# Adding gathered rows inside the gather's own transfer, in the second layer of a graph network

## The reference, cut to what matters

```python
h = max(layernorm(x), 0)
x = x + L0(h, edges)          # attention over edges; L0 itself returns h + agg @ Wo.T + bo
h = max(layernorm(x), 0)
x = x + L1(h, edges)          # weighted graph convolution, then two dense layers
# in L1: msgs = (h @ W)[dst] * norm, summed over the edges of each src
```

## Time and profile before

| | |
|---|---|
| median of 3 runs | 1908.72 us (1906.43 to 1911.76) |
| the profiled execution | 1886.7 us, of which the span from first to last instruction is 1885.1 us |
| stage 1 (about 183 to 710 us of the span) | PE nearly always busy |
| stage 2 (about 712 to 1066 us) | 25 quads |
| stage 3 (about 1066 to 1885 us) | PE nearly always busy |
| granted TensorE clock, mean | 0.931 of full speed |

### The profile page before, as it was taken

One profiled execution on the slowest core, in us unless ns is written; L12 is line 12 of the kernel. 1 busy time (PEld: TensorE's weight loads), 2 busy tenths in 40 slices (PEclk: granted clock), 3 DMA queues, 4 the chain that ended last, 5 costly groups with the idle time before them and its releaser, 6 DMA issues.

```text
span 1885.1 us, 30557 instructions
## 1 busy us (share of the span) xinstructions
PE 1625.4 (86%) x6531; PEld 1087.2 (58%) x6531; DVE 1430.1 (76%) x5731; ACT 1185.6 (63%) x2297; POOL 1216.8 (65%) x849
## 2 busy tenths in 40 slices
PE   4927999999999985676675349999999999999999
PEld 2314666666666653454454126666666666666666
DVE  7955777777777747877776487888888888888873
ACT  4924666666666631222222268899998989899984
POOL 2032888878788736888887765666666666666660
PEclk9967999999999997878878669999999999999999
DMA  6996666666666664655556589999999999999981
GB/s 231 418 404 235 182 179 183 194 181 177 193 188 178 176 189 101 123 109 108 119 107 136 96 199 263 249 268 264 271 270 270 269 267 271 268 270 271 270 234 75
DMA packets 150749, 398.56 MB, mean 211 GB/s; under 512 B 21586, under 2 KB 60060, under 8 KB 150700
## 3 DMA queue, kind: packets, MB, share of 16 engines
q1 hardware_dynamic: 89388, 264.75, 41.7%
q0 software_dynamic: 56416, 115.46, 32.5%
q10 hardware_dynamic: 4896, 17.83, 2.4%
HBM read 217.73 MB, written 180.23 MB: 211 GB/s over the span
## 4 chain that ended last, share of the span: by engine, by line
PE 51%; POOL 23%; DMA 8%; DVE 7%; issue 6%; SPq 1%; ACTq 1%; ACT 1%; POOLq 0%; DVEq 0%
PE bank L1314 9%; POOL sums_dram L514 9%; PE bank L1427 8%; PE bank L1416 8%; POOL kept L588 5%; PE bank L1321 5%; DMA out_dram<-cg 4%; PE bank L1351 4%; PE bank L1307 4%; POOL b_rs L510 4%; POOL cg L518 4%; PE bank L1255 4%; DVE cg L984 3%; DMA sums_dram<-ub,sidx 2%; PE bank L1295 2%
## 5 line engine op out<-in xcount | busy, mean ns | idle before, releaser
L1416 PE MATMUL bank<-kept,w 128*128 128x512 f32 x784 | 356.4, 598 | 0.0
L1427 PE MATMUL bank<-w_sb,kept 128*128 128x256 f32 x1568 | 354.3, 379 | 0.0
L588 POOL TENSOR_TENSOR kept<-kept 128x1024 f32<-128x1024 f32 x98 | 232.2, 2370 | 180.5 <-DVE cg L984 180.5
L1427 PEld LDWEIGHTS bank<-w_sb,kept 128*128 128x128 f32 x1568 | 297.9, 190 | 81.9 <-issue 46.4
L514 POOL DMA_INDIRECT sums_dram<-ub,sidx x148 | 243.1, 1643 | 76.8 <-issue 43.0
L1380 PE MATMUL bank<-cg,en 128*128 128x256 f32 x386 | 131.7, 485 | 124.1 <-ACT cg L1153 62.2
L510 POOL TENSOR_TENSOR b_rs<-b_ve,minus_half 128x8 f32<-128x8 f32 x102 | 208.7, 2047 | 28.7 <-DVE b_ve L1001 28.7
L1416 PEld LDWEIGHTS bank<-kept,w 128*128 128x128 f32 x784 | 142.8, 192 | 143.1 <-issue 143.0
L1191 ACT ACTIVATE kept<-kept,b_nb,b_rs 128x256 f32<-128x256 f32 x392 | 202.3, 589 | 21.5 <-DVE b_nb L974 21.5
L1181 ACT ACTIVATE kept<-kept,b_nb,b_rs 128x256 f32<-128x256 f32 x392 | 202.3, 589 | 11.0 <-DVE b_nb L974 11.0
L1314 PE MATMUL bank<-qkv_w,zT 128*128 128x512 f32 x392 | 192.7, 614 | 19.0 <-ACT zT L1070 19.0
(11 more groups left out here) (200 smaller groups left out, 3362.2 us busy)
## 6 DMA issues: line engine op xcount, KB each, us to landing
sums_dram<-cg SPq DMA_DIRECT2D x162, 512.0 KB, 5.4
kept<-in_x_dram SPq DMA_DIRECT2D x97, 512.0 KB, 5.7
kept<-sums_dram POOLq DMA_DIRECT2D x97, 512.0 KB, 10.0
cg<-sums_dram SPq DMA_DIRECT2D x97, 512.0 KB, 8.6
out_dram<-cg SPq DMA_DIRECT2D x97, 512.0 KB, 9.8
sums_dram<-cg ACTq DMA_DIRECT2D x34, 512.0 KB, 8.5
row_d<-in_dst_dram SPq DMA_DIRECT2D x48, 128.0 KB, 3.6
row_k<-keys_dram SPq DMA_DIRECT2D x24, 256.0 KB, 4.6
```

The costliest lines, as they stand in the source:

```text
L588: pool.tensor_tensor(X1[k.slot(8)], X[k.slot(4)], H[k.slot(2)], ALU.add).then_inc(g_xh, 1)
L1416: ins = pe.matmul(bank[:, 2 + m, :], w01[:, c, m * P:(m + 1) * P], hT[k.slot(2)][:, c * GN:(c + 1) * GN], start=(c == 0), stop=(c == KC - 1))
L1427: ins = pe.matmul(to, rT[k.slot(2)][:, c * GN + j * P:c * GN + (j + 1) * P], w2_sb[:, c, :], start=False, stop=(c == KC - 1), skip_group_c ...
```

## The change

The four gathers of a quad write straight onto `kept[:, Q*p + i, :]` as accumulating indirect DMAs. `C0` is no longer written or read. DVE still waits for the gathers' semaphore at the same place, then raises `n_x1` by itself instead of through the addition.

```diff
@@ -514,6 +514,10 @@
                 pool.indirect_dma_start(sums, bass.IndirectOffsetOnAxis(idx, 0), rows, None,
                                         bounds_check=bound, compute_op=ALU.add).then_inc(done, 16)
 
+            def gather_add(to, table, idx, bound, done):
+                pool.indirect_dma_start(to, None, table, bass.IndirectOffsetOnAxis(idx, 0), bounds_check=bound,
+                                        compute_op=ALU.add).then_inc(done, 16)
+
             def gather(to, table, idx, bound, done):
                 pool.indirect_dma_start(to, None, table, bass.IndirectOffsetOnAxis(idx, 0), bounds_check=bound,
                                         oob_is_err=True).then_inc(done, 16)
@@ -562,7 +566,7 @@
                     if p >= 2:
                         pool.wait_ge(n_x1, p - 1)
                     for i in range(chunks(Step(p))):
-                        gather(C0[p % 2][:, i, :], sums0, node_i[:, Q * p + i, 0:1], last_row, n_c0[p % 2])
+                        gather_add(kept[:, Q * p + i, :], sums0, node_i[:, Q * p + i, 0:1], last_row, n_c0[p % 2])
                 k = p - 2
                 if 0 <= k < NQ:
                     pool.wait_ge(n_UB, k + 1)
@@ -908,8 +912,7 @@
                         dve.wait_ge(n_c0[q], 16 * Q * (a.off // 2) + 16 * n)
                     else:
                         dve.wait_ge(n_c0[q], a.turns(2, 16 * Q))
-                    dve.tensor_tensor(quad(kept, a, slice(None)), quad(kept, a, slice(None)), C0[q][:, 0:n, :],
-                                      ALU.add).then_inc(n_x1, 1)
+                    dve.sem_inc(n_x1)
                     dve.wait_ge(n_sel, a.value(1))
                     dve.tensor_tensor(quad(norm, a), quad(found, a), quad(ew_f, a), ALU.mult).then_inc(n_norm, 1)
                     pass_on(dve, (n_x1, a.value(1)))
```

## The result

The changed kernel takes 1931.0 us (median of 4 runs, 1927.3 to 1935.7) against 1907.9 for the kernel before on the same chip: a ratio of 1.0132, 95% interval 1.0113 to 1.0150. That is some 25 us slower; the two medians alone are 23 us apart. The forecast was slower, +33 us and 1942 us, with a range of 1893 to 1958.

A forecast was written before the change was run, and what follows sets the result against it. POOL's issuing of indirect DMAs was taken to bound stage 2. Dearer gathers (+44.4 us) less cheaper scatters (12.9), plus 1.3 at the start and 0.4 at the end, gave +33.2 us: 1942 us, range 1893 to 1958.

The forecast's parts named there:

- What bounds the stage: Stage 2 is bound by how fast POOL issues indirect DMAs: 8 a quad, 13.93 us a quad.
- The gather's price: Stage 2, POOL: each accumulating gather takes 1.64 us, 0.555 us more for each of 80 gathers, 44.4 us.
- Rival 3: The accumulation costs part of it, the new gather taking 1.2 to 1.45 us: 1904 to 1927 us; chance 0.09.
- rival 1: The accumulating gather costs POOL no more than the plain one, so only savings are left: -14.5 us, 1894 us; chance 0.17.
- The scatters' saving: Stage 2, POOL: without the DVE addition the scatters' mean falls from 1.781 to about 1.62 us, 12.9 us saved.
- The start and the end: Stage 2's first quad costs +1.3 us; its last quad, after the steady stretch, +0.4 us.
- Sum: 31.5 us in the stretch, 1.3 at the start and 0.4 at the end: +33.2 us, 1942 us.
- Rival 2: Another DVE instruction, the counting L902, takes the addition's place in holding POOL: +46 us, 1955 us; chance 0.13.
- Rival 4: The landings of gathers or scatters become the bound, a few us a quad: +60 us, 1969 us; chance 0.03.

The follow-up runs named there:

- plain scatter: Kernel before, with the scatters of stage 2 into `sums1` writing their rows instead of accumulating them: 1876.3 us, ratio 0.9833.
- run with both: Changed kernel, with DVE still doing an addition of the same shape (`kept + kept` into the unused `C0`): 1932.6 us, ratio 1.0139.
- one input: Kernel before, its DVE addition L911 replaced by three statistics instructions of one SBUF input each, results unused: 1885.4 us, ratio 0.9887.
- split addition: Kernel before, its DVE addition L911 cut into four instructions of 256 elements, same result: 1881.5 us, ratio 0.9876.
- longer code: Kernel before, with 30 tiny DVE memsets put in front of stage 2 that compute nothing: 1875.7 us, ratio 0.9925.
- phase: Changed kernel plus an unused DVE addition placed some 1.2 us later, behind two unused statistics instructions: 1923.9 us, ratio 1.0166 to the kernel before.
- changed kernel with longer code: Changed kernel, with 30 tiny DVE memsets put in front of stage 2: 1929.5 us, ratio 1.0107 to the kernel before.
- half accumulating: Kernel before, with two of a quad's four gathers accumulating onto `kept`, two plain and added by DVE: 1892.1 us, ratio 1.0003.

## Why the prediction was right, and where it was off

**What bounds the stage: right.** POOL's issues and gaps fill it before and after, and the changed kernel's step moved by only 0.1 us when DVE got gaps of 6 us.

**The gather's price: right in kind, 6% too high.** Taken as 1.64 us from the accumulating scatter, it measured 1.608: +41.7 us instead of +44.4. The plain scatter (1.01 us) shows that the choice was the right one: the accumulation is what costs. Rival 3, a price between 1.2 and 1.45 us, falls with this number. With it falls rival 1, and with it what would have followed from the Trainium skill, DMA: Bandwidth & Descriptors, section Anatomy of one DMA, that many descriptors can be emitted before the incremental cost shows up; on an engine without idle time, 0.52 us for each gather showed at once.

**The scatters' saving: right in size, half right in its reason.** Taken as 12.9 us, measured 15.6. The prediction's 1.62 us kept the first scatter of a step at 1.62 and the last at 1.72; they came to 1.57 and 1.67. But the prediction put it down to the addition's absence. That is true of the kernel before (15.1 us on the scatters without it). In the changed kernel the addition would have cost nothing had it stayed, as the run with both shows: the longer steps had moved it. So this term belongs to the gathers' new timing as much as to the missing instruction.

**The start and the end: right.** First scatter 24.2 us after the first gather instead of 22.6, +1.6 against 1.3 predicted; from the last of the 20 quads to stage 3, 56.8 against 57.5 us, -0.7 against +0.4. The second number is within the spread: the unchanged kernel's second profile has 56.7 at the end.

**Sum.** 41.7 - 15.6 = 26.1 in the stretch, and 26.1 + 1.6 - 0.7 = 27 us (26.7 with the 0.3 us less in the gaps) against 33.2. What was off is the pair of mis-sized terms in the steady stretch, 2.7 us each and in the same direction; the rest is the end. Stage 3 kept its length (817.5 against 818.5 in the unchanged kernel's second profile).

**Rival 2** (L902 takes the addition's place) had a little to it: the third gather of a step takes 1.75 us in the mean where its neighbours take 1.56. That is 0.2 us a step and is within the 1.608. **Rival 4** (landings) did not come up: POOL has no idle time.

## What to carry to other kernels

Before moving an addition into a DMA, look at who issues it: an accumulating indirect DMA of 128 rows cost POOL 1.56 us here against 1.05 for the plain one, and on a queue without idle time that is paid in full, while the 1.23 us on DVE that it replaced had been hidden. Where one engine issues DMAs without pause, a long instruction of another that holds it is worth cutting up: four additions of 256 elements in place of one of 1024 gave 24 us (1.2%) with the same result, 16 of them in this stage, where the change cost 25. And a hold that depends on phase must be tested by moving the instruction, not only by removing it.

## What was not expected of the hardware

- The addition, with its two SBUF inputs on DVE, holds a DMA that POOL begins to issue after it. The edge is sharp: an issue 0.03 us after the addition's start was not held, one 0.06 us after it was, for all that was left of the addition, to within some 0.2 us. An issue that had already begun went on undisturbed: at 740.36 the whole addition lay beside one that took 1.58 us. The edge is not the same for each instruction: with the two longer ones of L902, issues up to 0.09 us after the start were not held and those from 0.10 us on were. Where an issue came just before the edge, DVE's instruction was the longer one (1.28 to 1.29 us for the addition instead of 1.23, 0.77 to 0.81 for L902 instead of 0.74).
- The Trainium skill, GPSIMD Engine Reference, section Key points, names the contention, with DVE instructions in a 2-port perf mode or with two SBUF inputs. The addition and L902 agree with it, and so do the statistics instructions and L885, which did not hold. L895 has one full SBUF input and held; which mode it runs in, no trace here shows.
- DVE stands still for 4.2 to 6.1 us where its loop of stage 3 first returns, in most kernels here; in the changed one:

```profile
1222.17 0.16 DVE L974 TENSOR_TENSOR b_rs<-b_rs,dinv 128x4 f32<-128x4 f32 x1 [5.74 <-issue]
```

  In five runs (one input, split addition, longer code, phase, and the changed kernel with longer code) DVE's program was longer ahead of that loop. All five lack this gap, and four of them have a stage 3 of 810 us instead of 814 to 818 (the phase run has 813). The half accumulating kernel, whose program is longer too but by less, has the gap (6.1 us). So part of the split addition's 24 us, an estimated 7 by what the memsets took from stage 3, comes with the place of the code and not with the addition. What exactly is slow at this return was not shown: the instruction queue has 34 packets in runs with the gap and in runs without it.
